# Masked scores in a contiguous buffer of their own, and new engine orders, in two attention layers of a four-part transformer kernel

## What is computed

```
for l in range(2):
    h = shift_token(x)                       # half the features from the token before
    q, k, v = split(h @ wqkv[l])             # 8 heads of 64
    q = l2norm(q) * qs;  k = l2norm(k) * ksc
    q, k = rotary_xpos(q, k)
    sim = einsum('bhwid,bhwjd->bhwij', 8 * q, look_around(k))   # windows of 128, this and the one before
    attn = softmax(where(mask, -max, sim))
    x = x + einsum('bhwij,bhwjd->bhwid', attn, look_around(v)) @ wo[l]
    a, g = split(layernorm(shift_token(x)) @ w1[l] + b1[l])
    x = x + (a * gelu(g)) @ w2[l] + b2[l]
```

## Time and profile before

| | us |
|---|---|
| median of 3 runs | 2405.11 (2396.6 to 2405.56) |
| profiled execution, its own time | 2403.95 |
| its span, first to last instruction | 2402.2 |
| PE busy | 2282.8 (95%) |
| DVE busy | 1790.3 (75%) |
| ACT busy | 1446.8 (60%) |
| POOL busy | 1290.5 (54%) |

### The profile page before, as it was taken

The page is one execution under the profiler, slowest core; times in us unless marked ns, Lnnn a source line. Parts: engine busy times, 40 slices in busy tenths (PEclk is TensorE's granted clock), DMA queues, the critical chain, the costliest instruction groups (busy, mean ns, idle before and its releaser), DMA issues. The chain is left out here.

```text
span 2402.2 us, 62203 instructions
## 1 busy us (share of the span) xinstructions
PE 2282.8 (95%) x22934; PEld 2038.9 (85%) x22934; DVE 1790.3 (75%) x5652; ACT 1446.8 (60%) x3631; POOL 1290.5 (54%) x1191
## 2 busy tenths in 40 slices
...
DMA packets 199074, 164.90 MB, mean 69 GB/s; under 512 B 22388, under 2 KB 189560, under 8 KB 197752
## 3 DMA queue, kind: packets, MB, share of 16 engines
...
## 5 line engine op out<-in xcount | busy, mean ns | idle before, releaser
L1280 POOL TENSOR_TENSOR b_sb_probs<-b_sb_probs,b_sb_r_sum 128x384 f32<-128x384 f32 x256 | 206.9, 829 | 272.1 <-DVE b_sb_r_sum L1509 271.9
L2034 POOL TENSOR_TENSOR c_kern_lo<-c_kern,c_kern_hi 128x512 fp32r<-128x512 f32 x128 | 179.0, 1399 | 300.8 <-ACT c_kern_hi L2128 300.8
L2128 ACT ACTIVATE c_kern_hi<-c_kern 128x512 fp32r<-128x512 f32 x128 | 80.9, 632 | 323.1 <-DVE c_kern L2248 323.1
L1363 ACT ACTIVATE b_sb_probs<-b_sb_probs,b_sb_neg_top 128x192 f32<-128x192 f32 x512 | 226.2, 445 | 4.8 <-DVE b_sb_neg_top L1481 4.1
L1481 DVE CUSTOM_DVE_ANT_0 b_sb_probs<-psum,b_sb_mask 128x192 f32<-128x192 f32 x512 | 151.2, 351 | 102.8 <-PE psum L1656 102.6
L46 PE MATMUL psum<-b_sb_fT_lo,b_sb_w_hi 128*128 128x256 f32 x704 | 206.0, 293 | 1.8 <-DVE b_sb_fT_lo L1549 1.4
L46 PE MATMUL psum<-c_kern_lo,c_v_hi 128*128 128x512 f32 x512 | 199.6, 390 | 0.2
L48 PE MATMUL psum<-c_kern_hi,c_v_hi 128*128 128x512 f32 x512 | 199.5, 390 | 0.0
L47 PE MATMUL psum<-c_kern_hi,c_v_lo 128*128 128x512 f32 x512 | 199.3, 389 | 0.0
L48 PE MATMUL psum<-b_sb_fT_hi,b_sb_w_hi 128*128 128x256 f32 x704 | 197.7, 281 | 0.0
L47 PE MATMUL psum<-b_sb_fT_hi,b_sb_w_lo 128*128 128x256 f32 x704 | 197.6, 281 | 0.0
...
## 6 DMA issues: line engine op xcount, KB each, us to landing
...
Y<-b_sb_y SPq DMA_DIRECT2D x128, 128.0 KB, 1.7
...
b_sb_v_far<-b_sb_v_own SPq DMA_DIRECT2D x128, 64.0 KB, 2.1
b_sb_x_f<-Y SPq DMA_DIRECT2D x128, 64.0 KB, 2.0
...
```

The source lines that it names most:

```text
L1280: pool.tensor_tensor(p, p, r, ALU.mult)\
L1363: ins = act.activation(probs[b][:, n // 2, :, n % 2, :], probs[b][:, n // 2, :, n % 2, :], ACT.Exp, bias=neg_top[b][:, n:n + 1], scale=-1. ...
L2034: pool.tensor_tensor(kern_lo[i % RING][:], kern[i % RING][:], kern_hi[i % RING][:].bitcast(F32), ALU.subtract)\
L2128: act.activation(kern_hi[i % RING][:], kern[i % RING][:], ACT.Copy).then_inc(hi_ready, 1)
```

## The change

The masked scores go to a new SBUF buffer `masked`, 8 heads of 192 columns for each b, contiguous for each head. `exps` reads from there and writes the exponentials into `probs` in the same strided rows as before. The lists of PE, DVE, ACT, SP and POOL for `layer_b` are replaced. They hold the same entries in a somewhat different order; PSUM's bank ring follows PE's list. Lines of the DVE part move down by one or two.

```diff
@@ layer_b
+        masked = [sb(f"masked{b}", [P, B_HEADS, B_SPAN]) for b in both]
         probs = [sb(f"probs{b}", [P, pairs, B_BLOCKS, 2, B_HALF]) for b in both]
@@ exps
-                    ins = act.activation(probs[b][:, n // 2, :, n % 2, :], probs[b][:, n // 2, :, n % 2, :], ACT.Exp, bias=neg_top[b][:, n:n + 1],
+                    ins = act.activation(probs[b][:, n // 2, :, n % 2, :],
+                                         masked[b][:, n, :].rearrange("p (i k) -> p i k", i=B_BLOCKS), ACT.Exp, bias=neg_top[b][:, n:n + 1],
                                          scale=-1.0, accum_out=row_sum[b][:, n:n + 1])
@@ top_of
-                    out=probs[b][:, m, :, j, :],
-                    in0=ring.out(t, (f"s{m}", b), 512)[:, j * B_SPAN:(j + 1) * B_SPAN].rearrange("p (i k) -> p i k", i=B_BLOCKS),
-                    in1=mask[:, min(t % NT, 1), :].rearrange("p (i k) -> p i k", i=B_BLOCKS), scale=-1.0, scalar=3.0e38, op0=ALU.add, op1=ALU.min,
+                    out=masked[b][:, n, :], in0=ring.out(t, (f"s{m}", b), 512)[:, j * B_SPAN:(j + 1) * B_SPAN],
+                    in1=mask[:, min(t % NT, 1), :], scale=-1.0, scalar=3.0e38, op0=ALU.add, op1=ALU.min,
@@ order (one line of the tables)
-        "pool": [("swap", 2, 9), ("swap", 3, 8), ("project_q", 0, 9), ("moments", 0, 7), ("project_k", 1, 9),
+        "pool": [("swap", 2, 9), ("swap", 3, 8), ("project_q", 0, 9), ("moments", 0, 7), ("project_k", 1, 9),
-                ("project_q", 1, 9), ("load_r", 0, 6), ("swap", 0, 10), ("rope", 0, 10), ("swap", 1, 10), ("swap", 4, 6),
+                ("project_q", 1, 9), ("rope", 0, 10), ("swap", 4, 6), ("scale", 0, 9), ("swap", 0, 10), ("load_r", 0, 6),
```

More of the change, by code:

```diff
@@ L918, in layer_b @@
     order = {
[L919 to L932, removed]
@@ new lines, in layer_b @@
+        "pe": [("scores2", 1, -1), ("down", 0, -4), ("project_k", 0, 0), ("turn_p", 0, -1), ("down", 1, -4),
+              ("project_q", 0, 0), ("turn_p2", 0, -1), ("project_k", 1, 0), ("turn_p", 1, -1), ("up", 2, -3),
+              ("turn_p2", 1, -1), ("up", 3, -3), ("values", 0, -1), ("values", 1, -1), ("project_q", 1, 0),
+              ("project_v", 0, 0), ("up", 4, -3), ("turn_h", 0, 1), ("up", 5, -3), ("project_v", 1, 0),
+              ("turn_f", 0, -2), ("bias", 0, 0), ("turn_qk", 0, 0), ("out", 1, -1), ("turn_h", 1, 1), ("scores", 0, 0),
+              ("scores2", 0, 0), ("out", 0, -1), ("turn_qk", 1, 0), ("up", 0, -2), ("up", 1, -2), ("scores", 1, 0)],
```

38 lines of the change are left out of this document (23 added, 15 removed).

## The result

The changed kernel takes 2413.4 us in the median of 8 runs (2407.16 to 2418.93), the kernel before 2398.86 beside it (8 runs, 2396.6 to 2405.76). The ratio is 1.0058, with a 95% interval of 1.0046 to 1.0070: some 14 us slower. The forecast was a small gain. The time lies inside its range, on the wrong side of no change.

A forecast was written before the change was run, and what follows sets the result against it. PE was taken to bound the layers. From 2403.95 us, -13.0 (old wait), +7.8 (new wait) and -1.3 (swap) gave 2397.5; the runs' median stands 1.2 higher, so 2398.6, said as 2398. The range was 2387 to 2414.

The forecast's parts named there:

- SP's list: SP's stores of `out` wait for `scores2(1)`, some 8 us later; `moments` reads their result 15 us after; cost nothing.
- The masked buffer: DVE's masking and ACT's exponentials with changed access pattern; costed at 0, bounds 0 to 1 us either way.
- Steps 1 to 6: Earlier reciprocals on DVE move POOL earlier, shorten DVE's clamps and end PE's wait at `project_q(1)`; -0.50 a step, -13.0 us.
- Step 3: PE's `down(1)` ahead of `project_q(0)` delays `sums_q(0)`: 0.33 us gain lost, 0.25 more; without POOL's gain +6.5 us.
- The new wait: PE's `scores(0)` waits for DVE's gating of `up(5)`, delayed by `norm` and `mid(3)`; 0.30 us a step, +7.8 us.
- rival C: Slower: `scores(0)` waits 1.1 us, with `norm`, the clamp of `spin_q(1)` and `mid(3)` all caught; 2419 us, chance 0.18.
- ACT's `turn_p2(1)`: On ACT, behind a table load and `up(2)`, ends near 1042.8, covered by 0.5 us before `values(1)`; cost nothing.
- POOL's `load_r`: On POOL, fills a gap behind `scale(0)`; cost nothing.
- The swap: At step 16, `swap_f(3)` leaves DVE's stretch and SP's `project_v(1)` stands 0.4 us earlier; -1.3 us, bounds -5 and +5.
- the signs: Expected profile: `turn_f` mark every 34.77 us, masking 351 ns, clamp's median falls, 26 waits at L1656; wrong outside 34.5 to 35.0.
- C's smaller half: The part of rival C with the smaller loss, up to which the range reached, 2414 us.

The follow-up runs named there:

- e6: The changed kernel with DVE's `mid(3)` back ahead of `turn_h(0)` and SP's list of before; 2387.26 us, ratio 0.9964.
- e4: The changed kernel with DVE's `mid(3)` back ahead of `turn_h(0)`; 2397.63 us, ratio 0.9998.
- e1: The kernel before with the masked buffer alone, all lists as before; 2398.48 us, ratio 1.0004.
- e3: The kernel before with, on DVE, `invert(1)` ahead of `down(0)` and `invert2(1)` ahead of `down(1)`; 2388.17 us, ratio 0.9962.
- e7: The kernel before with PE's new list: `down(1)` ahead of `project_q(0)`, `up(5)` ahead of `project_v(1)`; 2407.29 us, ratio 1.0044.
- e5: The kernel before with SP's new list alone; 2410.5 us, ratio 1.0048.
- e11: e6 with SP's weight loads `swap(0)` and `swap_f(2)` moved behind `project_v(1)`; 2379.83 us, ratio 0.9926.
- e2: The changed kernel's new lists alone, scores written into `probs` as before; 2410.6 us, ratio 1.0062 against the kernel before.

## Why the prediction was wrong

**The ladder.** The runs put a price on each part, in a chain of kernels, in us of 2398; by the intervals of the ratios each price is good to some 4 us. Before to e6 (all the new lists but SP's and `mid(3)`'s place, with the buffer): -8.6. e6 to e4 (SP's new list): +8.2. e4 to after (`mid(3)` late): +14.4. The sum is +14.0; measured was +14. The parts don't have fixed prices, though: SP's list costs 11.5 alone and 8.2 here, and DVE's delay shows only where PE's bank ring lets it.

**The masked buffer: right.** 0, by e1, with the interval of the ratio between -2 and +4 us. The row of the first layer's masking was the right one to read it from.

**Steps 1 to 6: right in mechanism, 0.40 for 0.50 and so 9 to 10 us for 13.** e3 shows the reciprocals, the earlier POOL, the shorter clamp and the vanished wait. I took the best end of the bounds, and 3 us are missing from it. I gave as the reason that three rows tie DVE's ends to POOL's to within 0.02 us; two do, the third ends 0.28 later. Step 3, the cost of `down(1)` ahead of `project_q(0)`, delays the sums as worked out, but costs nothing, even without the earlier POOL: in e7 the shorter clamp behind them takes it back. So the +6.5 us of the bound was too much. e6, which has `down(1)` first, and e3, which has not, have the same period (34.55 and 34.56).

**The new wait: right in place, wrong in size.** This is one of the two steps that failed. I had +0.30 a step, from `norm` held "up to 1.0 us" and `mid(3)` 0.8 more. `mid(3)` came as worked out (held 1.12 beyond its start, ending 0.27 after POOL's sum). `norm` did not: it consists of two instructions, and POOL has a sum and a product nearly back to back. I let the first collide and forgot that the second then starts into the product. 1.78 us more, not 1.0. With it the idle time in that step is 0.71 and the delay 0.81, where I had 0.30. That is rival C's condition, the wait above 0.50, met in another way than C said: the clamp of `spin_q(1)` wasn't caught, `norm` was caught twice. The trace of before had all that was needed: the two instructions of `norm`, and POOL's product 0.15 us behind its sum (1048.81 to 1050.10, then 1050.25 to 1051.29), which the earlier trace rows leave out. Not every step pays the 0.81 (the waits are 0.53 in the mean); the ladder puts the term at +14.4 us where the sum had +7.8. With that alone the sum would be 2403.95 - 13.0 + 14.4 - 1.3 = 2404.1, no change. It takes the 4.4 us missing from the gain (8.6 for 13.0) and SP's 8.2 to make the kernel slower.

**SP's list: wrong, "nothing" for 8 to 12 us.** This is the other step. I asked who reads what the stores of `out` write (`moments`, 15 us later) and not what stands behind them in the queue. `load_f` waits there for their landing, the store of `down(1)` behind `load_f`, and DVE for that store, 1.24 us in the step shown, 27.8 us in 22 waits. The instruction moved was late by 6 us at no cost of its own; its neighbours in the queue paid. The price is that of the whole list (e5, e6). That the store of `down(1)` makes it is read from the traces, and the longer waits for v, whose moves stand behind `load_f` too, are a part of it.

**ACT's `turn_p2(1)` and POOL's `load_r`: not contradicted.** No wait at `values` names ACT. The waits there name v and DVE's rotation ahead of `turn_p(1)`, that is `spin_k(1)`, and go with SP's list (e4 against e6).

**The swap: wrong sign, small.** The waits for v grew from 4.6 to 8.5 us where I had -1.3. The seven steps around the swap take 257.3 us by the marks against 256.8 before, and the five of the earlier trace rows 186.7 against 184.5. One of them took 41.0 us against 36.7: in it `down(1)` waited 4.9 us for its store, and PE 4.1 us for DVE behind that. Ordering v ahead of the weights is worth 6.6 us there (e6 against e11), which no part of the change did.

**The range and the signs.** 2413.4 stands at the edge of my range (2414), where "C's smaller half" had it, and that it stands inside is luck. The range was laid about a median of 2405.11 from three runs; eight runs give 2398.86. As a change the range reached from -18 to +9 us, and +14 is outside it. The ratio's interval is 0.12% to either side, some 3 us, not the 12 that I thought could be told. C had too small a chance beside a forecast that rested on a difference of 0.30 against 0.50. Of the signs, the period of 35.41 has left 34.5 to 35.0, which I had named as a sign of being wrong. The masking, the exponentials and the clamp (median 263 ns after, 631 before) came as said, and the wait at L1656 (now L1657) came 23 times for 26.

**What stays open.** The layer's length accounts for 10.5 of the 14 us in the one pair of profiles. The profiled execution of after is the fastest of its eight, and e2, with the same lists, has a length of 1088.7. So the rest is likely a spread of the waits from run to run, but no run separates it. Also, the period after is 35.41 in one profile while single even steps are 34.6 to 35.9 long; which steps get the shorter form was not traced.
